# A layer of three blocks on one core: two gate products placed earlier on TensorE, six delta sums moved to GpSimd, and three mask products moved to VectorE

## What is computed

```
xi, z = jnp.split(x @ in_w.T, 2, axis=-1)
xc = jax.nn.silu(conv_b + sum((xp[:, k:k + L, :] * conv_w[:, k] for k in range(dc))))
dt, Bm, Cm = split(xc @ xproj_w.T)
delta = jax.nn.softplus(dt @ dt_w.T + dt_b)
dA = jnp.exp(delta[..., None] * A)
dBu = delta[..., None] * Bm[:, :, None, :] * xc[..., None]
h = da * h + dbu;  y = einsum('bdn,bn->bd', h, c)          # over the tokens
y = ys.swapaxes(0, 1) + xc * D_skip
return y * jax.nn.silu(z) @ out_w.T
```

## Time and profile before

| | us |
|---|---|
| median of three runs | 495.16 (494.64 to 495.6) |
| the profiled execution | 495.07 |
| its span | 493.3 |
| TensorE busy | 444.8 (90%) |
| VectorE busy | 375.1 (76%) |
| ScalarE busy | 238.7 (48%) |
| GpSimd busy | 165.3 (34%) |
| share of the chain that ended last | PE 63%, DVE 12%, issue 7%, SPq 6%, DMA 5%, ACT 4% |

### The profile page before, as it was taken

One profiled execution on the slowest core, in us unless ns is written; L12 is line 12 of the kernel. 1 busy time (PEld: TensorE's weight loads), 2 busy tenths in 40 slices (PEclk: granted clock), 3 DMA queues, 4 the chain that ended last, 5 costly groups with the idle time before them and its releaser, 6 DMA issues.

```text
span 493.3 us, 6895 instructions
## 1 busy us (share of the span) xinstructions
PE 444.8 (90%) x1817; PEld 220.2 (45%) x1817; DVE 375.1 (76%) x712; ACT 238.7 (48%) x422; POOL 165.3 (34%) x161
## 2 busy tenths in 40 slices
PE   8999999999999989898579758898889889799997
PEld 3554655655554557654345402122222222285654
DVE  0257586565666677597979988999999999988756
ACT  1143323112221333289667856788888888531100
POOL 5000000100100020307700026798989898331000
PEclk9999999999999999999989957999999999999999
DMA  6992029200000000220254656456555755520000
GB/s 203 344 320 88 1 95 319 85 1 0 0 2 0 0 1 0 77 85 17 65 149 124 171 147 176 133 155 202 162 153 160 203 164 150 156 73 13 11 11 23
DMA packets 36596, 52.28 MB, mean 106 GB/s; under 512 B 5952, under 2 KB 26956, under 8 KB 36572
## 3 DMA queue, kind: packets, MB, share of 16 engines
q1 hardware_dynamic: 35420, 50.79, 34.9%
q10 hardware_dynamic: 1152, 1.19, 0.8%
HBM read 35.08 MB, written 16.52 MB: 105 GB/s over the span
## 4 chain that ended last, share of the span: by engine, by line
PE 63%; DVE 12%; issue 7%; SPq 6%; DMA 5%; ACT 4%; POOL 1%; DVEq 0%; POOLq 0%; ACTq 0%
PE ps L327 14%; PE ps L399 12%; PE ps L2107 7%; PE ps L1750 4%; PE ps L2074 4%; PE ps L1030 3%; DMA brows<-bparts 3%; PE ps L1703 3%; PE ps L1725 2%; DMA area<-in_xT 2%; PE ps L1716 2%; PE ps L348 2%; DVE da L1929 2%; DVE rc L1391 2%; SPq L1552 1%
## 5 line engine op out<-in xcount | busy, mean ns | idle before, releaser
L1898 POOL TENSOR_TENSOR gb<-da,hb 128x512 f32<-128x512 f32 x62 | 77.7, 1274 | 62.7 <-ACT da L1818 56.4
L1818 ACT ACTIVATE da<-da 128x512 f32<-128x512 f32 x128 | 79.0, 629 | 21.7 <-DVE da L1929 19.2
L1929 DVE TENSOR_TENSOR da<-ps,expA 128x512 f32<-128x512 f32 x128 | 84.1, 686 | 6.5 <-PE ps L1703 5.7
L327 PE MATMUL ps<-area,convw 128*128 128x384 f32 (+1 forms) x220 | 73.4, 486 | 0.7 <-DMA area<-in_xT 0.7
L399 PE MATMUL ps<-wall,peT 128*128 128x512 f32 x144 | 67.7, 593 | 0.0
L1703 PE MATMUL ps<-drows,selb 96*128 96x512 bf16 x128 | 48.7, 402 | 12.1 <-DVE da L1929 5.0
L327 PEld LDWEIGHTS ps<-area,convw 128*128 128x128 f32 (+1 forms) x220 | 41.2, 190 | 28.5 <-issue 1.4
L587 ACT ACTIVATE kvs<-ps 128x512 f32<-128x512 f32 x36 | 21.5, 597 | 52.6 <-PE ps L399 52.6
L1716 PE MATMUL ps<-urows,brows 96*128 96x512 bf16 x96 | 35.4, 398 | 10.0 <-DVE gb L1936 7.0
L579 ACT ACTIVATE peT<-ps 128x384 f32<-128x384 f32 x24 | 11.8, 491 | 65.5 <-PE ps L327 58.9
L1703 PEld LDWEIGHTS ps<-drows,selb 96*128 96x128 bf16 x128 | 11.3, 98 | 62.5 <-DVE da L1929 51.2
(11 more groups left out here) (247 smaller groups left out, 760.8 us busy)
## 6 DMA issues: line engine op xcount, KB each, us to landing
area<-in_xT SPq DMA_DIRECT2D x11, 768.0 KB
yscr<-inw SPq DMA_DIRECT2D x28, 208.0 KB
brows<-bparts SPq DMA_DIRECT2D x16, 240.0 KB, 2.9
dparts<-pt SPq DMA_DIRECT2D x21, 128.0 KB, 2.4
drows<-dparts SPq DMA_DIRECT2D x14, 192.0 KB, 2.9
uparts<-pt SPq DMA_DIRECT2D x18, 128.0 KB, 2.4
urows<-uparts SPq DMA_DIRECT2D x15, 144.0 KB, 2.9
inw<-in_in_wT SPq DMA_DIRECT2D x2, 1024.0 KB, 8.1
```

Of the source, the lines that this page charges most:

```text
L327: mm = pe.matmul(bank(T_EMB + j % 2, 0, EN), convw[0:n, k, h * P:(h + 1) * P], xbuf[0:n, q, k, c * EN:(c + 1) * EN], start=(k == 0), stop= ...
L1818: act.activation(da_at(q, j), da_at(q, j), ACT.Exp, scale=-1.0).then_inc(da_ready, 1)
L1898: pool.tensor_tensor(gb_at(q, j), da_at(q, j), state, ALU.mult).then_inc({2: m2_done, 3: m3_done, 4: m4_done}[s_], 1)
L1929: dve.tensor_tensor(da_at(q, j), bank(j % 2), expA[:, j % 2, :], ALU.mult).then_inc(e_free, 1)
```

## The change

Four things are changed, all in the preparation. (1) TensorE does z(0) and z(1) right after `xt(0)`, into the banks 4 and 5, which `above(0)` and `above(1)` have freed, and the later z move up by the places that this leaves; `xt(3)`, `xt(4)` and `xt(5)` stand before the `dt_product` that they stood behind. `dt_product(5)` waits for ScalarE's copy of z(1). (2) GpSimd does the sums `delta_(n)` of items 2, 3, 4, 7, 8 and 9 (`BY_POOL`); it clears `drows` between the two threes. (3) VectorE does direction 1's three products of B's parts with the mask (`spread`), placed after `lost(3)`, `lost(4)` and `above(4)`. (4) The order on VectorE and ScalarE is fitted to it: `lost(5)` to `lost(8)` stand before `rest(n)`, items 8 and 9 are both treated at item 4, and ScalarE's copies and gates stand elsewhere.

```diff
@@ -972,6 +972,7 @@
         STEPS = [(0, 0), (0, 1), (0, 2), (1, 0), (1, 1), (0, 3), (1, 2), (1, 3), (0, 4), (1, 4)]
         ITEMS = [(d, k if d == 0 else L - 1 - k) for d, k in STEPS]
         NI = len(ITEMS)
+        BY_POOL = [(2, 3, 4), (7, 8, 9)]
 
         def step(n):
             return STEPS[n][1]
@@ -996,7 +997,7 @@
         BC_BANK, DT_SLOT, BC_SLOT = [0, 2], [1, 3], [0, 0]
         BC_COPIED = [7, 10]
         ZS = [8, 3, 1, 7, 2, 4, 5, 6]
-        Z_BANK = [6, 7, 6, 7, 4, 5, 6, 7]
+        Z_BANK = [4, 5, 6, 7, 4, 5, 6, 7]
         NEZ = len(EARLY)
         XI_AT = [1024 * slot + (NE * B if n < DC else 0) for n, slot in enumerate(XI_SLOT)]
         CD_SLOT = [3, 3]
@@ -1108,9 +1109,14 @@
             bc(1)
             pe.wait_ge(diag_ready, 2)
             xt(0)
+            pe.wait_ge(rc_ready, 1)
+            z(0)
+            pe.wait_ge(rc_ready, 2)
+            z(1)
             pe.wait_ge(bct_ready, 2)
             pe.wait_ge(rc_ready, 3)
             xt(1)
+            pe.wait_ge(z_copied, NEZ + 2)
             dt_product(5)
             dt_product(6)
             pe.wait_ge(rc_ready, 5)
@@ -1118,22 +1124,18 @@
             xt(2)
             pe.wait_ge(CT_ready, 1)
             spread_c(1)
-            pe.wait_ge(CT_ready, 2)
-            z(0)
+            xt(3)
             pe.wait_ge(rc_ready, 6)
             dt_product(7)
-            xt(3)
-            z(1)
+            pe.wait_ge(CT_ready, 2)
+            z(2)
+            xt(4)
             pe.wait_ge(rc_ready, 7)
             dt_product(8)
-            xt(4)
-            pe.wait_ge(z_copied, NEZ + 1)
-            z(2)
+            z(3)
+            xt(5)
             pe.wait_ge(rc_ready, 8)
             dt_product(9)
-            xt(5)
-            pe.wait_ge(z_copied, NEZ + 2)
-            z(3)
             pe.wait_ge(rc_ready, 9)
             z(4)
             xt(6)
@@ -1260,24 +1262,25 @@
             for n in range(2):
                 logarithm(n)
             b_middle(1)
-            for n in range(2, 5):
-                logarithm(n)
+            silu_z(0, ACT.Copy)
+            logarithm(2)
+            logarithm(3)
+            silu_z(1, ACT.Copy)
+            logarithm(4)
             high(0)
+            copy_cd(0)
             softplus_terms(5)
-            copy_cd(0)
             middle(0)
+            high(1)
             softplus_terms(6)
-            high(1)
             middle(1)
             copy_cd(1)
+            high(2)
             softplus_terms(7)
-            high(2)
             middle(2)
-            silu_z(0, ACT.Copy)
+            high(3)
             softplus_terms(8)
-            high(3)
             middle(3)
-            silu_z(1, ACT.Copy)
             softplus_terms(9)
             logarithm(5)
             high(4)
@@ -1287,16 +1290,16 @@
                 logarithm(n)
             high(5)
             silu_z(2)
+            middle(5)
+            high(6)
             silu_z(3)
-            middle(5)
+            middle(6)
             silu_z(4)
-            high(6)
+            high(7)
             silu_z(5)
-            middle(6)
-            high(7)
-            silu_z(6)
             middle(7)
             high(8)
+            silu_z(6)
             silu_z(7)
             store(act, 7)
             middle(8)
@@ -1319,12 +1322,15 @@
             def b_rest(d):
                 pool.wait_ge(bhi_ready, d + 1)
                 pool.tensor_tensor(brest[:, d, :, :], bct[:, d, :, 0:NS], bshi[:, d, :, :], ALU.subtract).then_inc(bres_ready, 1)
-                spread(bhi[:, d, :], bshi[:, d, :, :]).then_inc(bd_ready, 1)
+                if d == 0:
+                    spread(bhi[:, d, :], bshi[:, d, :, :]).then_inc(bd_ready, 1)
 
             def b_low(d):
                 pool.wait_ge(bmi_ready, d + 1)
                 pool.wait_ge(bres_ready, d + 1)
                 pool.tensor_tensor(bslo[:, d, :, :], brest[:, d, :, :], bsmi[:, d, :, :], ALU.subtract).then_inc(bslo_ready, 1)
+                if d == 1:
+                    return
                 spread(bmi[:, d, :], bsmi[:, d, :, :]).then_inc(bd_ready, 1)
                 pool.wait_ge(bslo_ready, d + 1)
                 spread(blo[:, d, :], bslo[:, d, :, :]).then_inc(bd_ready, 1)
@@ -1347,6 +1353,23 @@
             b_rest(1)
             b_low(1)
             c_spread(1)
+
+            def delta_(n):
+                q = n % 2
+                pool.wait_ge(ln_ready, n + 1)
+                pool.wait_ge(rc_ready, n + 1)
+                pool.wait_ge(hi_ready, n - 1)
+                pool.wait_ge(res_ready, n - 1)
+                pool.tensor_tensor(du[:, q, 0, :], rc[:, n % NZ, :], ez[:, n % NZ, :], ALU.add).then_inc(delta_ready, 1)
+
+            for n in BY_POOL[0]:
+                delta_(n)
+            pool.wait_ge(xc_ready, 2 * DC)
+            pool.wait_ge(bc_ready, 2)
+            for q in range(2):
+                pool.memset(drows[0:KS // 2, q, :], 0.0).then_inc(cleared, 1)
+            for n in BY_POOL[1]:
+                delta_(n)
 
         def prepare_vector(dve):
             ch = Chain(dve, d_chain, links[0])
@@ -1448,33 +1471,45 @@
             bc_copied(1)
             lost(1)
             above(1)
-            for some in ((2, 3), (4,)):
-                for n in some:
-                    plus_one(n)
-                for n in some:
-                    lost(n)
-                for n in some:
-                    above(n)
-            NEXT = {1: (5,), 2: (6,), 3: (7, 8), 4: (9,)}
+            mask4 = maskb[:, :, :].unsqueeze(1).to_broadcast([P, L, GB, NS])
+            def spread(dst, src, ready, n):
+                dve.wait_ge(ready, 2)
+                dve.wait_ge(bd_ready, n)
+                dve.tensor_tensor(dst[:, 1, :].rearrange("p (t g n) -> p t g n", t=L, g=GB),
+                                  src[:, 1, :, :].unsqueeze(2).to_broadcast([P, L, GB, NS]), mask4,
+                                  ALU.mult).then_inc(bd_ready, 1)
+
+            for n in (2, 3):
+                plus_one(n)
+            for n in (2, 3):
+                lost(n)
+            spread(bhi, bshi, bhi_ready, 3)
+            for n in (2, 3):
+                above(n)
+            plus_one(4)
+            lost(4)
+            spread(bmi, bsmi, bmi_ready, 4)
+            above(4)
+            spread(blo, bslo, bslo_ready, 5)
+            NEXT = {1: (5,), 2: (6,), 3: (7,), 4: (8, 9)}
             delta_(0)
             u_(0)
             for n in range(NI):
                 more = NEXT.get(n, ())
-                if n not in (4, NI - 1):
+                for m in more[:1]:
+                    lost(m)
+                if n in (0, 5):
                     delta_(n + 1)
                 rest(n)
                 if n not in (4, NI - 1):
                     u_(n + 1)
-                for m in more[:1]:
-                    lost(m)
                 skip_(n)
                 for m in more[:1]:
                     above(m)
                 for m in more[1:]:
                     lost(m)
+                    above(m)
                 low(n)
-                for m in more[1:]:
-                    above(m)
                 if n == 0:
                     ch.upto(c_dot_b(1))
                 if n == 4:
@@ -1874,11 +1909,6 @@
             send_y(act, ylast, NG - 1, 1, (0, 1))
 
         def scan_gpsimd(pool):
-            pool.wait_ge(xc_ready, 2 * DC)
-            pool.wait_ge(bc_ready, 2)
-            for q in range(2):
-                pool.memset(drows[0:KS // 2, q, :], 0.0).then_inc(cleared, 1)
-
             def decayed(g, q, s_, d):
                 j = 2 * (s_ - 1) + d
                 pool.wait_ge(da_ready, 8 * g + j + 1)
```

## The result

The changed kernel took 490.19 us (median of 6 runs, 489.68 to 492.94), the kernel before beside it 494.94 us (6 runs). The ratio is 0.9902, with a 95% interval of 0.9875 to 0.9930. That is -4.75 us, where -3.34 was forecast (491.7, range 489.3 to 494.0). The profiled execution took 490.11 us with a span of 488.2.

The account below looks back on a forecast made before the run. The prediction took the kernel to be bound by SyncE's queue, started by the end of VectorE's low(8) at 284.78 us. Terms -3.34 - 0.5 + 0.1 - 1.2 + 0.4 + 0.8 + 0.4 = -3.34 us gave 491.7 us, range 489.3 to 494.0.

Parts of the forecast that it names:

- The hole: VectorE's idle before u(3), waiting for TensorE's late xt(3); early gate products remove it whole, -3.34 us.
- the exclusion of VectorE and GpSimd: VectorE reading two SBUF operands stands still while GpSimd works, write-only GpSimd instructions excepted; the second to issue blocks fully.
- The masks: Three mask products moved to VectorE: 2.75 us of standstills removed, 2.2 us of work added; net -0.5 us (-1.0 to +0.6).
- Up to `rest(2)`: VectorE loses two sums, gains lost(6), and meets GpSimd's product for C and sum 2; together +0.1 us.
- From `u(3)` to `delta(5)`: VectorE loses delta(4), lost(6) and a wait before u(4), gains some 0.3 us of waiting; net -1.2 us.
- From `delta(5)` to the end of `low(8)`: Three sums leave VectorE, -1.8; a wait before u(7), overlaps and TensorE's steps come in; net +0.4 us.
- The clock: TensorE's clock may fall again from 251 to 255 us, slowing z(2), dt_product(8) and z(3); +0.8 us (0 to 1.6).
- Handovers: Passing four waited-for sums between VectorE and GpSimd, 0.1 us each; +0.4 us (0 to 1.2).
- rival (b): Gain of 5 to 6 us: clock stays up, GpSimd's sums fall beside u and skip; 489.6 us, chance 0.12.
- part 2: Direction 1's three mask products moved from GpSimd to VectorE; net -0.5 us (-1.0 to +0.6).
- Rival (c): No change: what is won before 285 us is given back in the scan's first groups; 495.0 us, chance 0.06.
- Rival (d): Slower: each of six GpSimd sums lies whole on VectorE's path through mutual blocking; 497.6 us, chance 0.07.

Follow-up runs that it names:

- z_only: Changed kernel with the masks back on GpSimd and all ten sums on VectorE, leaving the early gate products and new orders; 491.30 us, ratio 0.9884.
- sums_only: Kernel before with only the six sums on GpSimd and VectorE's order that goes with them, masks on GpSimd, gate products late; 495.65 us, ratio 0.9991.
- masks_only: Kernel before with only direction 1's three mask products moved to VectorE, gate products late; 496.30 us, ratio 1.0013.
- z_masks: Changed kernel with all ten sums on VectorE; gate products early, masks on VectorE; 491.53 us, ratio 0.9901.
- probe_ms: Changed kernel with eight idle GpSimd memsets added between its memsets and sum 7; length from plus_one(0) to the end of low(8) 53.65 us.
- probe_tt: Changed kernel with four idle GpSimd additions of two SBUF operands added between its memsets and sum 7; 492.37 us (median of 3).
- z_sums: Changed kernel with direction 1's three mask products back on GpSimd; gate products early, six sums on GpSimd; 490.87 us, ratio 0.9880.

## Why the prediction was right

The direction was right, and so was the mechanism: the hole, and the exclusion of VectorE and GpSimd. The sum was 1.4 us short of the median and 1.8 short of the traces. Term by term, from the two profiles:

- *The hole*, -3.34: gone whole, as forecast. What it is worth by itself, with the new orders, is 3.83 us in z_only, for this has no wait before `u(2)` and `u(4)` either. It is not a fixed size: in sums_only, with the clock up, the hole was 1.64 us.
- *The masks*, -0.5: `delta(0)` at 238.79 instead of 239.33, -0.54. The price taken for a mask, 0.73 us to the next start, was 0.74 (233.73 to 234.47). Taken out in the experiments they are worth 0.70 us of the length without and 0.44 with the sums on GpSimd.
- *Up to `rest(2)`*, +0.1: from `delta(0)` to `u(3)` 12.98 us for 13.51, so -0.53. Mis-sized: sum 2 held `low(0)` for 0.47 us, not 0.7, `delta(1)` stood 1.77 for 1.92, and `u(2)` no longer waited for `xt(2)`.
- *From `u(3)` to `delta(5)`*, -1.2: 12.45 us for 13.88, -1.43.
- *From `delta(5)` to the end of `low(8)`*, +0.4: 15.40 for 14.72, +0.68. The sign was right: the last three sums cost more than they save. But the wait did not stand before `u(7)`, as said; it stood inside `rest(6)`, which sum 7 held up by 1.07 us, and `low(6)`, by 0.82. `low(7)` took 0.13 longer, and `u(9)` waited 0.36 us.
- *The clock*, +0.8: 0. It stayed up in 252 to 256, and z(2) took 1.88 us. This is the largest term of the miss. The price was misread too: the 2.74 us taken for a gate product at half clock is one across the change, and one wholly at 0.50 took 3.78 (masks_only). Even so no run shows the upper end of 1.6 us behind early gate products. In z_masks the clock did stay down (the columns are those of the earlier trace rows):

```profile
248.00:252.00 4.00, 3.49 (x14) 2.98 (x15) 4.00 (x6) 2.52 (x3) 0.00 (x0) 0.50 0.20 55
```

There `xt(3)` took 2.83 us instead of 1.59 and ended at 251.34, still 1.11 us before `u(3)` began, and VectorE waited nowhere longer than in z_only. In probe_ms, at 0.55, it waited 0.32 us more. The forecast left this slack of TensorE out.

- *Handovers*, +0.4: 0. No row priced them, and no run shows them. Sum 3 starts 0.16 us behind the end of `rest(1)`, and nobody was waiting for it, nor for sums 2 and 4.

-3.34 - 0.54 - 0.53 - 1.43 + 0.68 = -5.16 us. In the traces that is rival (b), a gain of 5 to 6 us with the clock up and sums beside `u` and `skip`, and `low(8)` came earlier than the 2.5 to 4.5 us that the forecast gave as its sign. By mechanism it is the forecast with its two allowances, 1.2 us, taken off and the term up to `rest(2)` 0.6 us better. The other signs held: the masks are shown at 0.81 and 0.82 us, the sums at 1.27 (sum 7 at 1.42), and SyncE's queue, from its first start behind `low(8)` to the issue of the u parts at the end of that chain, takes 8.46 us for 8.45. The range of 489.3 to 494.0, in which 490.19 lies, does not follow from the outer values named for it: part 2, the clock and the handovers, added straight to 491.7, give 490.0 to 494.4.

Rival (c) falls by the 208.6 us behind `low(8)` and by the median. Rival (d) names a real price: in probe_tt the three VectorE instructions that met an addition took 0.58, 1.07 and 1.07 us longer, and sums 7 to 9 cost more than they save. It did not decide, since sums 2 to 4 mostly fell beside `u`, `skip` and `above`.

## What to carry to other kernels

Moving an operation from VectorE to GpSimd pays where it lands beside VectorE instructions that read PSUM, and costs up to its whole length where VectorE wants two operands from SBUF: read what VectorE does in that very slot before moving anything (here three sums won 1.3 us of the stretch and three like them lost 0.7). An instruction that is longer than its like by an odd amount, and ends by its own usual time behind the end of the other engine's instruction (0.55 us at 512 columns, 1.09 at 1024), is the sign to look for; taking work off GpSimd and giving it to VectorE can then be a gain for VectorE. A hole on one engine hides what is won in front of it, so it is closed first: in masks_only VectorE reached the hole 1.41 us earlier than before and left it 0.20 us later. And where several engines' orders change at once, the device time may not show the smaller parts; a length between two instructions, here steady to 0.02 us, does.

## What the runs showed of the hardware

The hindrance goes both ways and in turns. Sum 7 took 1.42 us for 1.27 behind a VectorE instruction, and in sums_only sum 8 took 2.02 us: it began at 275.71, beside `low(6)`, and ended at 277.73, 1.21 us after VectorE had gone on to `rest(7)`, which in turn ended 0.55 us behind it:

```profile
275.38 1.21 DVE L1458 TENSOR_TENSOR pt<-res 128x1024 bf16<-128x1024 f32 x1
276.52 1.76 DVE L1443 TENSOR_TENSOR res<-du 128x512 f32<-128x512 f32 x1
```

In probe_tt the shortest of the four additions took 1.27 us and the longest 1.60; VectorE got one two-operand instruction in between each two of the last three.

Two operands from SBUF are not the only case. `plus_one(4)` reads a single operand and takes 0.41 us, but beside GpSimd's mask product it took 0.75 us before and in z_sums.

The time that TensorE's clock takes from such a stretch is a matter of which work it hits: the same gate product took 1.88 to 1.98 us with the clock up, 2.74 across the change and 3.78 at a granted clock of 0.50. Three profiles of the changed kernel show the same 53.33 to 53.35 us from `plus_one(0)` to `low(8)`, though in one of them that stretch starts 2.6 us later (at 228.85 for 226.29), and the span behind it differs by 1.2 us. So in these three the differences arise before and behind the stretch that was changed, not in it; for the scatter of its 18 times, 489.1 to 493.1 us, that is likely but not shown.
